# A sparse graph layer: chunks of 2048 columns folded within themselves, and the diagonal left in the search

## The reference, cut to what matters

```python
h = jnp.maximum(layernorm(x), 0.0)                    # x: 8192 x 512
mask = adj > 0                                        # adj: 8192 x 8192, nearly all zeros
head = mask / jnp.maximum(jnp.sqrt(jnp.sum(mask * mask, -1, keepdims=True)), 1e-12)
inc = adj + head
out = x + (inc @ h) / jnp.sum(inc, -1, keepdims=True)
```

## Time and profile before

| | |
|---|---|
| median of three runs | 1272.74 us |
| the runs | 1274.66, 1272.74, 1272.05 us |
| span of the profiled execution | 1276.7 us |
| DVE busy | 1189.2 us (93%) |
| ACT busy | 975.5 us (76%) |
| PE busy | 959.0 us (75%) |
| GpSimd busy | 791.1 us (62%) |
| moved by DMA | 471.00 MB, 369 GB/s over the span |

### The profile page before, as it was taken

The page is one execution under the profiler, slowest core; times in us unless marked ns, Lnnn a source line. Parts: engine busy times, 40 slices in busy tenths (PEclk is TensorE's granted clock), DMA queues, the critical chain, the costliest instruction groups (busy, mean ns, idle before and its releaser), DMA issues.

```text
span 1276.7 us, 14660 instructions
## 1 busy us (share of the span) xinstructions
PE 959.0 (75%) x2680; PEld 478.1 (37%) x2682; DVE 1189.2 (93%) x2868; ACT 975.5 (76%) x1902; POOL 791.1 (62%) x748
## 2 busy tenths in 40 slices
PE   0003878888888878787988887978878888977677
PEld 0001434444444444443434443434444434433343
DVE  6679999998999999998999999999999999999961
ACT  6657787887887988786888877888877888884731
POOL 1003667676666777776766767777776776765562
PEclk9999899898988989899898989999989988987888
DMA  9999999999999999999999999999999999997532
GB/s 356 427 422 406 396 394 388 369 387 369 379 378 382 401 373 401 395 401 394 402 400 401 392 374 384 399 400 395 402 396 402 402 397 373 401 390 275 175 106 74
DMA packets 148207, 471.00 MB, mean 369 GB/s; under 512 B 24826, under 2 KB 24826, under 8 KB 143965
## 3 DMA queue, kind: packets, MB, share of 16 engines
q1 hardware_dynamic: 90368, 331.38, 66.3%
q0 software_dynamic: 57744, 138.64, 29.7%
HBM read 490.47 MB, written 33.82 MB: 411 GB/s over the span
## 4 chain that ended last, share of the span: by engine, by line
DVE 55%; issue 17%; DMA 11%; ACT 6%; PE 6%; another core or an unknown queue 2%; SPq 1%; POOL 0%; DVEq 0%; ACTq 0%; POOLq 0%
DVE cand_word L794 17%; DVE folded L772 16%; DMA adj_tile<-in_adj_dram 8%; DVE cand_index L798 6%; DMA gathered_rows<-in_x_dram 3%; PE acc L1326 3%; DVE cand_index L817 2%; DVE cand_word L812 2%; ACT junk L573 2%; ACT adj_tile L560 2%; ACT diag L636 1%; PE acc L1337 1%; DVE diagonal_alone L779 1%; DVE entry L961 1%
## 5 line engine op out<-in xcount | busy, mean ns | idle before, releaser
L494 POOL DMA_INDIRECT gathered_rows<-h_scratch,slot_column x520 | 559.9, 1077 | 263.1 <-issue 158.0
L573 ACT ACTIVATE junk<-adj_tile,zero_unit 128x2048 bf16<-128x2048 f32 x256 | 510.0, 1998 | 48.3 <-issue 27.5
L1326 PE MATMUL acc<-gathered_rows,diag 128*128 128x512 f32 x1040 | 489.6, 622 | 21.4 <-DMA gathered_rows<-h_scratch,slot_column 18.2
L494 POOL DMA_INDIRECT gathered_rows<-h_scratch,spill_column x198 | 223.1, 1127 | 195.0 <-ACT spill_column L619 135.2
L794 DVE MAX8 cand_word<-folded 128x8 f32<-128x1024 f32 x244 | 298.2, 1222 | 5.9 <-remote 1.3
L772 DVE SCALAR_TENSOR_TENSOR folded<-adj_tile 128x1024 f32<-128x1024 f32 x244 | 296.1, 1214 | 7.7 <-DMA adj_tile<-in_adj_dram 5.6
L1326 PEld LDWEIGHTS acc<-gathered_rows,diag 128*128 128x128 f32 x1040 | 203.8, 204 | 263.4 <-issue 262.6
L798 DVE FIND_INDEX8 cand_index<-cand_word,folded 128x8 uint32<-128x1024 f32 x244 | 297.3, 1219 | 0.0
L1337 PE MATMUL acc<-gathered_rows,spill_matrix 128*128 128x512 f32 x396 | 186.8, 609 | 46.0 <-DMA gathered_rows<-h_scratch,spill_column 42.4
L636 ACT ACTIVATE diag<-ident,weights_and_payload 128x128 f32<-128x128 f32 x581 | 176.2, 388 | 16.0 <-issue 6.5
L1337 PEld LDWEIGHTS acc<-gathered_rows,spill_matrix 128*128 128x128 f32 x396 | 72.8, 192 | 154.8 <-issue 154.6
(11 more groups left out here) (151 smaller groups left out, 880.1 us busy)
## 6 DMA issues: line engine op xcount, KB each, us to landing
adj_tile<-in_adj_dram SPq DMA_DIRECT2D x256, 1024.0 KB
h_scratch<-adj_tile SPq DMA_DIRECT2D x16, 1024.0 KB, 10.6
out_dram<-out_tile SPq DMA_DIRECT2D x64, 256.0 KB
gathered_rows<-in_x_dram SPq DMA_DIRECT2D x12, 1024.0 KB, 12.6
x_residual<-in_x_dram SPq DMA_DIRECT2D x48, 256.0 KB
gathered_rows<-h_scratch,slot_column POOLq DMA_INDIRECT x520
x_held<-in_x_dram SPq DMA_DIRECT2D x4, 1024.0 KB, 7.9
gathered_rows<-h_scratch,spill_column POOLq DMA_INDIRECT x198, 3.5
```

The lines of the kernel that those rows point to most:

```text
L494: nc.gpsimd.indirect_dma_start(out=into, out_offset=None, in_=h[:, :], in_offset=bass.IndirectOffsetOnAxis(ap=column, axis=0), bounds_chec ...
L573: nc.scalar.activation(junk[:, n % 2].rearrange("p (j c) -> p j c", j=2), both[:, :, half], ACT.Relu, bias=zero_unit[:], scale=-UP, accum_ ...
L1326: last = nc.tensor.matmul(acc[t % 3][:], diag[:, t % 2, 1 + s], slot(t % 2, s), start=False, stop=False)
```

## The change

A chunk is now 2048 adjacent columns of a row, so a lane reads one run of 8 KB; its first 1024 columns are the left part of the fold and the other 1024 the right part. `read_diagonal`, `cut_diagonal` and `keep_diagonal` are gone. The diagonal takes part in the search like any entry. When a tile's columns are known, `find_diagonal` looks through the 8 places of the one chunk that can hold it, compares their columns with the lane's own row number (modulo 2048), and puts the match into the place of the diagonal; `leave_diagonal` subtracts it from the list. `columns_any` moves ahead, next to `values`; `counts` and `ranks` move back by one fold and one search operation each.

```diff
-    adj_h = adj.rearrange("(c p j) (h n) -> c j p h n", p=P, j=ROWS, h=2)
+    adj_t = adj.rearrange("(c p j) n -> c j p n", p=P, j=ROWS)
...
         def diag_chunk(t):
-            return t // ROWS * P * ROWS % HALF // CW
+            return t // ROWS * P * ROWS // (2 * CW)
...
                         sp.wait_ge(folded, CHUNKS * (t - 2) + j + 1)
-                        if j == diag_chunk(t - 2):
-                            sp.wait_ge(diag_read, t - 1)
-                sp.dma_start(chunk(t % 2, j), adj_h[t // ROWS, t % ROWS, :, :, CW * j:CW * (j + 1)]).then_inc(adj_loaded[t % 2][j], 16)
+                sp.dma_start(A[:, t % 2, 2 * CW * j:2 * CW * (j + 1)],
+                             adj_t[t // ROWS, t % ROWS, :, 2 * CW * j:2 * CW * (j + 1)]).then_inc(adj_loaded[t % 2][j], 16)
...
-                if j == diag_chunk(t):
-                    read_diagonal(t)
-                    cut_diagonal(t)
...
-            def keep_diagonal(t):
-                dve.wait_ge(diag_read, min(t, FOLDED - 1) + 1)
-                nc.vector.tensor_copy(val[:, 0:1], on_diag[:, t:t + 1]).then_inc(diag_kept, 1)
+            def in_diag_chunk(ap, t):
+                return ap[:, 0:CAND].rearrange("p (e s) -> p s e", s=CHUNKS)[:, diag_chunk(t)]
+
+            def find_diagonal(t):
+                dve.wait_ge(cola_ready, t + 1)
+                dve.wait_ge(val_ready, t + 1)
+                nc.vector.scalar_tensor_tensor(out=own_entry[:], in0=in_diag_chunk(cola, t), scalar=diag_column(t),
+                                               in1=in_diag_chunk(val[:, 1:], t), op0=ALU.is_equal, op1=ALU.mult,
+                                               accum_out=val[:, 0:1]).then_inc(diag_found, 1)
+
+            def leave_diagonal(t):
+                dve.wait_ge(diag_found, t + 1)
+                rest = in_diag_chunk(val[:, 1:], t)
+                nc.vector.tensor_tensor(rest, rest, own_entry[:], ALU.subtract).then_inc(diag_left, 1)
...
                 find_values(t, 0)
                 if small:
                     values(p)
-                    keep_diagonal(p)
+                    columns_any(p)
...
                 find_places(t, 0)
                 if small:
-                    counts(p)
+                    find_diagonal(p)
                 if pick:
                     take_entry(r)
                 fold(t, 1)
                 if small:
-                    columns_any(p)
-                    ranks(p)
+                    leave_diagonal(p)
                 if pick:
                     sum_entry(r)
                 find_values(t, 1)
                 if small:
+                    counts(p)
+                find_places(t, 1)
+                if small:
+                    ranks(p)
                     columns(p)
-                find_places(t, 1)
                 if small:
                     own_columns(p)
                     pay_columns(p)
```

More of the change, by code:

```diff
@@ L205, in chunk, with diag_column @@
             return A[:, b, 2 * CW * j:2 * CW * (j + 1)].rearrange("p (h c) -> p h c", h=2)
-        def diag_half(t):
-            return t // ROWS * P * ROWS // HALF
         def diag_chunk(t):
-            return t // ROWS * P * ROWS % HALF // CW
-        def diagonal(row, t):
-            first = t // ROWS * P * ROWS % CW
-            return row[:, first:first + P * ROWS].rearrange("p (m j) -> p j m", j=ROWS)[:, t % ROWS]
+            return t // ROWS * P * ROWS // (2 * CW)
+        def diag_column(t):
+            return diag_at[:, t % 16:t % 16 + 1]
         def cands(t):
@@ L247, in searched @@
             return CHUNKS * min(t, FOLDED) + PARTS * max(t - FOLDED, 0)
-        def part(i):
-            return i % 2 * CHUNKS + i // 2
         def paid(t, k):
@@ L467, in _ @@
             on_diagonal(ident[:], 0, 1.0)
-            step(nc.gpsimd.memset(cap[:], 3.0e38))
-            on_diagonal(cap[:], 0, 0.0)
-            step(nc.gpsimd.memset(on_diag[:, FOLDED:BATCH + 1], 0.0))
             step(nc.gpsimd.memset(ones[:], 1.0))
@@ L773, in fold @@
                                                op0=ALU.mult, op1=ALU.add).then_inc(folded, 1)
-                if j == diag_chunk(t):
-                    read_diagonal(t)
-                    cut_diagonal(t)
-            def read_diagonal(t):
-                nc.vector.scalar_tensor_tensor(out=picked[:], in0=diagonal(chunk(t % 2, diag_chunk(t))[:, diag_half(t)], t),
-                                               scalar=1.0, in1=ident[:], op0=ALU.mult, op1=ALU.mult,
-                                               accum_out=on_diag[:, t:t + 1]).then_inc(diag_read, 1)
-            def cut_diagonal(t):
-                words = diagonal(F[:, diag_chunk(t) % 2], t)
-                dve.wait_ge(folded, CHUNKS * t + diag_chunk(t) + 1)
-                nc.vector.tensor_tensor(words, words, cap[:], ALU.min).then_inc(diag_cut, 1)
             def find_values(t, j):
                 dve.wait_ge(folded, CHUNKS * t + j + 1)
-                if j == diag_chunk(t):
-                    dve.wait_ge(diag_cut, t + 1)
                 nc.vector.max(out=cv[:, t % 2, 8 * j:8 * j + 8], in_=F[:, j % 2]).then_inc(vals_found, 1)
@@ L801, in part_columns @@
             def part_columns(t, i):
-                if t == BATCH:
-                    return A[:, 0, CW * part(i):CW * (part(i) + 1)]
-                return chunk(t % 2, part(i) % CHUNKS)[:, part(i) // CHUNKS]
+                return A[:, t % 2, CW * i:CW * (i + 1)]
             def part_values(t, i):
@@ L809, in part_values @@
                 else:
-                    dve.wait_ge(adj_loaded[t % 2][part(i) % CHUNKS], 16 * turn(t))
-                e = slice(8 * part(i), 8 * part(i) + 8)
+                    dve.wait_ge(adj_loaded[t % 2][i // 2], 16 * turn(t))
+                e = slice(8 * i, 8 * i + 8)
                 nc.vector.max(out=cv[:, t % 2, e], in_=part_columns(t, i)).then_inc(vals_found, 1)
@@ L864, in columns_any @@
                 dve.wait_ge(idx_found, searched(t) + searches(t))
-                nc.vector.scalar_tensor_tensor(out=ranked(cola[:], t), in0=ranked(ge[:], t), scalar=float(HALF),
+                nc.vector.scalar_tensor_tensor(out=ranked(cola[:], t), in0=ranked(ge[:], t), scalar=float(CW),
                                                in1=by_rank(ci[:, t % 2], t), op0=ALU.mult,
@@ L1035, in count_bad @@
                                                     op0=ALU.mult, op1=ALU.add))
-                step(nc.vector.scalar_tensor_tensor(out=z_right[:, on_right], in0=right_diag[:], scalar=ZERO,
-                                                    in1=z_right[:, on_right], op0=ALU.mult, op1=ALU.add))
                 step(nc.vector.tensor_scalar(well[:], z_left[:], ZERO * HALF, None, ALU.is_equal))
@@ L1073, in wide_period @@
                 part_values(t, 0)
+                if p == FOLDED:
+                    no_diagonal()
                 tell_halves(p)
@@ L1077, in wide_period @@
                 values(p)
-                keep_diagonal(p)
+                columns_any(p)
                 part_values(t, 1)
                 find_entry(r)
+                if not wide(p):
+                    find_diagonal(p)
                 part_places(t, 1)
+                if not wide(p):
+                    leave_diagonal(p)
+                take_entry(r)
                 counts(p)
-                take_entry(r)
                 if t == FOLDED + 1:
@@ L1122, in batch_period @@
                 values(y)
-                keep_diagonal(y)
                 sum_entry(v)
@@ L1189, in drain @@
                 values(z)
-                keep_diagonal(z)
                 counts(z)
```

24 lines of the change are left out of this document (11 added, 13 removed).

## The result

The changed kernel takes **1696.97 us** (median of four runs, 1690.33 to 1699.20) against 1273.40 of the kernel before (four runs, 1272.05 to 1274.66): a ratio of 1.332, 95% interval 1.330 to 1.335. The prediction was 1258.6 us, 1243 to 1277. It was wrong by 438 us.

A forecast was written before the change was run, and what follows sets the result against it. The prediction took DVE to set the pace of most tiles and DMA that of the last ones. Savings of 5.6 + 7.0 - 2.6 + 3.6 + 0.5 = 14.1 us gave 1258.6 us, range 1243 to 1277.

The forecast's parts named there:

- the part on DMA: Loads of `adj`: bytes stay, tiles keep their form with at most 383 of 384 shared places, 0.2 us a tile saved.
- 8 KB in place of 4: Loads of `adj` in longer runs: 0.16 to 0.28 us less a tile, 0.2 taken, ends 0 and 0.28.
- 394 becomes 399: DMA's rate in GB/s in the folded stage, raised by the 0.2 us, 1.2% of a tile, from longer runs.
- Longer packets push the gathers back: Gathers' share of DMA falls from 39% to 29%, PE waits 0.6 us in 45 tiles: 1294 us, chance 0.05.
- DVE's terms: DVE's small steps: 0.67 us a tile removed, less 0.07, 0.13 and 0.10 for new operations and order, 0.37 saved.
- the term of the order: On DVE, `own_columns` straight behind `columns`, on which it waits: 0.10 us a tile, ends 0 and 0.14.
- the term of 0.37: DVE's net saving in us for each folded tile, between 0.13 and 0.55, making its pace 16.63 us.
- The cushion: 3.6 MB of loads running ahead keep DVE's pace for 19 tiles from tile 16, 7.0 us saved; then DMA paces.
- the rival in which the runs bring nothing: Loads of `adj` get no faster, DMA stays at 394 GB/s, DVE's pace lasts 13 tiles: 1267.8 us, chance 0.17.
- Late counts: `ranks` 2.5 us later in the tile delays PE and loads; at 0.4 us a tile 18 us lost: 1277, chance 0.17.

The follow-up runs named there:

- e1: The changed kernel with room for 512 shared places in the batch in place of 384: 1290.01 us, ratio 1.012.
- e2: The kernel before with the batch's limit set to 272 shared places: 1477.04 us, ratio 1.158.
- e3: The kernel before with chunks of 2048 adjacent columns alone, diagonal still cut out behind the fold: 1278.94 us, ratio 1.0045.
- e5: e1 with `find_diagonal`, `leave_diagonal`, `counts` and `ranks` as early as the columns allow: 1288.60 us, ratio 1.011.
- e8: e1 with each chunk's two parts apart in SBUF, so its 8 KB runs move in pieces of 4 KB: 1271.25 us, ratio 0.9993.
- e6: e4 with `find_diagonal`, `leave_diagonal`, `counts` and `ranks` as early as the columns allow: 1273.89 us, ratio 1.0013.
- e7: The kernel before with `counts`, `ranks` and `columns` as late as in the change: 1276.07 us, ratio 1.0030.
- e4: The changed kernel's search and order, with the old chunks of two 4 KB runs: 1273.00 us, ratio 0.9991.
- e10: e8 with only 64 of the 512 columns of `x` loaded from tile 18 on: 1250.45 us, ratio 0.983.
- e13: The kernel before with only 64 of the 512 columns of `x` loaded from tile 18 on: 1263.57 us, ratio 0.993.
- e12: e8 with a lane's 8 KB of a folded tile moved in four pieces of 2 KB: 1305.80 us, ratio 1.025.

## Why the prediction was wrong

**The failed step** is the sentence in the part on DMA: "A count on the inputs gives 319 shared places a tile in place of 277, at most 383 of the 384, so the tiles keep their form." The count was right for the 61 folded tiles and stopped there. The rows that fail their test go on to the batch, which has the same limit of 384, and there 58 rows in place of 51 want 413 places in place of 282. Four dense passes at 104.3 us are 417 us, of 424 that the kernel lost; e1 and e2 show the limit as the cause from both sides. No rival had it: all of them were about times, none about which branch the data take.

**The runs, alone and beside the gathers.** The term "8 KB in place of 4" was sized from loads alone, and there it held: 418 predicted to become 425 or 430, measured 426, in e3 434. The step from there to "394 becomes 399" failed. Beside the gathers the profiled executions with 8 KB pieces moved 390 (the changed kernel), 393 (e5) and 395 GB/s (e3), and ACT waited only 3.3, 4.0 and 9.9 us for loads: the faster loads were there, and the gathers paid for them. Three pairs with 8 and with 4 KB pieces say the same in times: e1 and e8 1290 and 1271, e5 and e6 1289 and 1274, e3 and the kernel before 1279 and 1273. The lower end of this term was set to 0 on the ground that the faster stretches have no gathers; that ground left room for an end below zero.

**Longer packets push the gathers back**, the rival with a chance of 0.05, is the one that came true in direction. Its sign in the trace ("PE waiting much longer for gathered rows") is there in each kernel with 8 KB pieces and goes with the pieces in e8. Its argument against, that loads stop when room is full and the gathers then have all, did not save them: from 95 to 1115 us SP waited 439.5 us for ACT's checks to free room (151.3 before), and the spill's gathers still landed 2 us later. Its 1294 us lies next to e1's 1290 by luck: it was worked out from the share that all of a tile's gathers get, 17.8 us for 2.10 MB, and what the trace shows is one gather that lands late in a loop with PE. The Trainium skill ("DMA: Bandwidth & Descriptors", Queues, rings and completion order) has each engine take the queues in turn. That would make it so; that the pieces' size does it is shown, the turns themselves no row shows.

**DVE's terms.** Over a tile without a stall (230.16 to 246.84 us of the changed kernel, beside 249.87 to 266.83 before), start to start: `find_diagonal` 0.14 (0.13 taken), `leave_diagonal` 0.08 (0.07), the three removed 0.65 (0.67), and `columns` with the wait behind it:

```profile
238.76 0.17 DVE L855 SCALAR_TENSOR_TENSOR column_less_base<-entry_sign,column_if_any 128x32 f32<-128x32 f32 x1
238.96 0.17 DVE L864 TENSOR_TENSOR slot_column<-column_less_base,slot_base 128x8 uint32<-128x8 f32 x1
```

0.20 from `columns` to `own_columns`, where before 0.12 stood behind it: 0.08 (0.10 taken). That gives 0.35; the pace shows 0.26 to 0.28. The rest is in other small steps that start a few hundredths later behind new neighbours (0.03 behind `counts`, 0.02 behind the sum of the entries, 0.02 behind `own_columns`), which the sum had at nothing. e7 measures the order by itself: its first folds of tiles 3 and 12, at 131.34 and 285.75 us, make 17.16 us a tile, 0.18 more than before, where the term of the order had 0.10 and an upper end of 0.14. So the term of 0.37 was 0.1 too large, inside its ends of 0.13 and 0.55.

**The cushion.** This step held in kind, and e8 is where to read it, as it has the saving without the gathers' waits. The prediction let DVE's pace last until tile 35 with faster runs, and until tile 29 without; e8 keeps 16.7 to tile 28:

```profile
548.18 1.22 DVE L760 SCALAR_TENSOR_TENSOR folded<-adj_tile 128x1024 f32<-128x1024 f32 x1
...
1108.92 1.22 DVE L760 SCALAR_TENSOR_TENSOR folded<-adj_tile 128x1024 f32<-128x1024 f32 x1
```

Then (1108.92 - 548.18) / 32 = 17.52 us a tile, against 17.2 in the forecast and 17.4 in the rival in which the runs bring nothing. That rival's 1267.8 is 3.5 us under e8's 1271.25. Most of the saving of the first 28 tiles is paid back in the last 32.

**Late counts** cost 3.4 us (e7), not the 18 that the rival had; the order of the small steps was the wrong place to fear. (`ranks` moved behind two searches, as that rival has it, and not by a fold and a search, as the section on the change says.)

**Still open:** why e1, e3 and e5, with 8 KB pieces, spread over 13 to 17 us from run to run where the kernels with 4 KB stay within 7. TensorE's clock is one candidate. From 340 to 1115 us PE took 3.9 us or more from the start of the spill's products to its next work, in place of 2.65, in 15 of 44 tiles of the changed kernel, 11 of 44 in e3 and 18 of 45 in e5, against none before and 5 of 45 in e4 and e8. And e3's two fastest runs (1270.97 and 1272.41 us) have the highest mean granted clock of its ten, 0.948, its two slowest (1283.80 and 1286.69) the lowest, 0.929 and 0.933. Whether the clock makes a run long or late gathers make the clock low, no run settles. Nor did a run take the product out of the loop, by putting `find_owner` ahead of `product_spill` in PE's list. The best version that computes all, e8, can't be told from the kernel before.

## What to carry to other kernels

- Where a change alters what passes a data-dependent test, count the inputs through every limit behind it, up to the last fallback, and look up how often that fallback would run and what one pass takes. One limit, 384 against 413, cost thirty times the gain that the sum had.
- A rate measured with one queue busy says little about two. Here, where bulk loads share the DMA engines with gathers that others wait for, the larger piece gave the faster load and the later gather; the size between was found by trying (8, 4 and 2 KB: 1290, 1271 and 1306 us).
- As far as these traces tell, a late gather cost nothing until the loop that it sits in was longer than DVE's tile. Add up such a loop (here gather, product, `find_owner`, `spill_column`, gather) beside the busiest engine's own sum.
- Before paying for a saving on an engine, take bytes away from the other candidate as a probe (e10, e13): it shows what the saving would be worth, here 13 us, and who keeps it.

## What the runs showed that I had not expected

- Piece size in both directions. Loads alone ran at 415, 416 to 421 and 426 to 434 GB/s with 2, 4 and 8 KB pieces; beside the gathers 380 to 960 us moved 380 with 2 KB (e12), 393 to 396 with 4 KB (e4, e6, e7, e8, the kernel before) and 390 to 395 with 8 KB (the changed kernel, e5, e3). In time the middle size won.
- The cut is set by the layout on the SBUF side as much as by the run in DRAM: with the same 8 KB runs, two destinations a lane make 32768 more packets (e8) and the kernel 19 us faster.
- The cost of late gathers shows mostly on other engines than the one that waits for them first: PE's waits grew by 40 us, ACT's for PE by 114.
